# Three mixtures of experts: all rows through all experts, or only the routed rows in blocks of 128

## The chip, the cores and the metric

One core of a Trainium2 chip runs the whole program. The metric is device time in microseconds of one execution. The engines are TensorE (PE, its weight loads PEld), VectorE (DVE), ScalarE (ACT), GpSimd (POOL) and SyncE (SP, which issues most DMAs). Each works through its own instruction stream and waits on semaphores that the others raise.

## The reference

The input x is 2 x 512 rows of 128 numbers, in float32; a context of 2 x 77 rows goes with it. Four levels follow, each adding a gated attention to the context (the second with a self-attention inside its feed-forward part) and a gated mixture of experts. The mixtures of levels 1 to 3 have 8 experts with 512 hidden units, and each row uses its two best experts:

```
gate_probs = softmax(x1 @ Wg + bg);  topk_p, topk_i = top_k(gate_probs, 2)
comb = sum(one_hot(topk_i, E) * topk_p[..., None], -2)          # level 1 divides topk_p by its sum
h = gelu(einsum('bsd,edf->bsef', x1, W1) + b1)
y = einsum('bsef,efd->bsed', h, W2) + b2
moe_out = einsum('bse,bsed->bsd', comb, y)
```

Level 2 has a ninth choice (the row itself, without an expert) and no biases; level 3 has the tanh form of gelu and plain probabilities as weights. The reference multiplies every row by every expert and lets `comb` put zeros on six of the eight.

## The kernel before

Rows lie in 8 tiles of 128, four for each batch ("half"). Each engine's stream is written out by hand; the order of the code is the order of the work, and semaphores hold the engines together. The stages are: level 0 (attention and a mixture of another kind), cross-attention 1, self-attention, mixture 1, cross-attention 2 ("attention 2"), mixture 2, attention 3, mixture 3.

A mixture (`moe`) runs 16 pairs of an expert and a half in the order `MOE_ORDER`. On PE, `hidden(i)` (L1527) multiplies the 512 turned rows of the half (HTR, feature by row) by the first matrix in four matmuls of 512 columns; ACT applies gelu (L689); then 16 matmuls (L1543) make the expert's output for four tiles, in one of two PSUM banks. DVE (L1087) adds it to ACC, times the row's gate (GC). `hidden(i+1)` is issued before the second matrices of pair i. The weights of an expert, 512 KB, are one slot of the ring RINGW of 6; SP (L360) loads the next when a slot is free, 8 experts for a mixture. Between the pairs, at the places PREPARE_AT, VW_AT and NEXT_AT, stand the keys and values of the next attention and the turn of its first half.

A cross-attention (`cross_tiles`) runs units of 8 heads on one tile, 16 in attentions 2 and 3, as a pipeline over PE, DVE, ACT and POOL (L477 divides by the sum); `before[s]` are steps of DVE on the second half that belong to the mixture before. In its last steps the first half is normalized and turned for the next mixture.

## Time and profile before

| what | value |
|---|---|
| median of 3 runs | 948.68 us (943.76 to 1962.34) |
| the profiled execution | 943.48 us |
| its span, first to last instruction | 941.7 us |
| busy PE / DVE / ACT / POOL | 766.1 / 462.1 / 395.4 / 137.1 us |
| mean granted clock of TensorE | 0.902 |
| DMA | 38.48 MB, mean 41 GB/s |

The profile is of one execution. Busy time is the union of an engine's instructions; a group's mean is that of one instruction, which overlaps its neighbours, so that the mean times the count exceeds the busy time. One float32 matmul of the program leaves two records. The granted clock is a share of 2.4 GHz: 1.00 is that level, 0.50 is 1.2 GHz.

### The profile page before, as it was taken

To read this page: it belongs to the slowest core of one execution; us is meant where nothing else is said; L and a number is where in the kernel's file an instruction comes from. 1 tells how busy PE (TensorE), PEld (TensorE's weight loads), DVE (VectorE), ACT (ScalarE), POOL (GpSimd) and SP (SyncE) were. 2 spreads that over 40 slices of the span, in tenths; PEclk is the share of its full clock that TensorE was granted. 3 is DMA by queue.
4 is the path that set the end of the run, shared out by engine and by line. 5 is a ranking of instruction groups with operands and counts; after the bars stand their busy time and mean duration, and the time that the engine had idled before them with its cause. 6 is when DMAs were issued, how large, how long until landed. Compare 5 with 4: busy or idle time off the path is not lost.

```text
span 941.7 us, 12265 instructions
## 1 busy us (share of the span) xinstructions
PE 766.1 (81%) x4480; PEld 507.0 (54%) x4480; DVE 462.1 (49%) x1144; ACT 395.4 (42%) x942; POOL 137.1 (15%) x205
## 2 busy tenths in 40 slices
PE   2042589856779999799999768999999678899997
PEld 2030246635542333267677446767777458677775
DVE  6977923277776775262113589341121448432112
...
GB/s 356 57 1 0 0 45 179 6 1 2 128 223 51 2 3 1 135 1 1 31 38 46 67 1 1 1 1 23 45 23 78 12 1 1 1 1 1 45 12 12
DMA packets 16802, 38.48 MB, mean 41 GB/s; under 512 B 1174, under 2 KB 10707, under 8 KB 16483
## 3 DMA queue, kind: packets, MB, share of 16 engines
...
q8 instruction: 36, 0.59, 0.3%
q14 instruction: 24, 0.20, 0.1%
...
## 4 chain that ended last, share of the span: by engine, by line
PE 66%; DVE 24%; ACT 5%; issue 4%; DMA 1%; POOL 0%; SPq 0%; DVEq 0%; ACTq 0%; POOLq 0%
PE PS L1543 18%; PE PS L1527 18%; PE PS L1659 4%; PE PS L1354 3%; PE PS L1621 3%; DVE NTOP L1030 3%; PE PS L1649 3%; DVE MX L1162 2%; DVE BIG L1031 2%; PE PS L1310 2%; PE PS L1260 1%; DVE XH L787 1%; PE PS L1364 1%; PE PS L1502 1%; PE PS L1340 1%
## 5 line engine op out<-in xcount | busy, mean ns | idle before, releaser
L1543 PEld LDWEIGHTS PS<-RINGW,BIG 128*128 128x128 f32 x1536 | 178.8, 192 | 22.0 <-issue 22.0
L1543 PE MATMUL PS<-RINGW,BIG 128*128 128x128 f32 x1536 | 179.3, 275 | 0.3 <-PE PS L1543 0.3
L1087 DVE SCALAR_TENSOR_TENSOR ACC<-PS,GC,ACC 128x128 f32<-128x128 f32 x192 | 54.1, 344 | 252.1 <-PE PS L1543 222.9
L1527 PE MATMUL PS<-HTR,RINGW 128*128 128x512 f32 x384 | 175.5, 602 | 2.6 <-PE PS L1543 1.5
L689 ACT ACTIVATE BIG<-PS,Wt 128x512 f32<-128x512 f32 x128 | 86.5, 685 | 89.0 <-PE PS L1527 88.6
L1527 PEld LDWEIGHTS PS<-HTR,RINGW 128*128 128x128 f32 x384 | 70.2, 192 | 76.1 <-issue 75.9
L1162 DVE TENSOR_REDUCE MX<-PS 128x2 f32<-128x1024 f32 x64 | 78.5, 1226 | 25.5 <-PE PS L1621 23.7
L1354 PE MATMUL PS<-BIG 128*128 128x128 f32 x400 | 56.6, 293 | 8.7 <-DVE TMP L1212 3.1
L477 POOL TENSOR_TENSOR BIG<-BIG,REC 128x616 f32<-128x616 f32 x40 | 48.6, 1215 | 94.6 <-DVE REC L1040 94.6
L1354 PEld LDWEIGHTS PS<-BIG 128*128 128x128 f32 x400 | 51.2, 203 | 17.6 <-issue 10.6
L689 ACT ACTIVATE BIG<-PS 128x512 f32<-128x512 f32 x64 | 37.9, 598 | 38.3 <-PE PS L1527 37.8
L1649 PE MATMUL PS<-BIG 75*128 75x512 bf16 x128 | 44.7, 406 | 6.7 <-ACT BIG L742 2.4
L1621 PE MATMUL PS<-BIG 72*128 72x512 bf16 x128 | 43.2, 429 | 4.8 <-DVE RK L1137 2.4
L594 ACT ACTIVATE BIG<-BIG 128x308 f32<-128x308 f32 x40 | 18.5, 463 | 59.4 <-DVE BIG L1031 59.2
L1030 DVE TENSOR_REDUCE NTOP<-PS 128x8 f32<-128x616 f32 x32 | 25.6, 800 | 35.2 <-PE PS L1340 29.0
L742 ACT ACTIVATE BIG<-PS 128x512 f32<-128x512 f32 x64 | 34.9, 595 | 15.7 <-PE PS L1649 15.1
L600 ACT ACTIVATE BIG<-PS,NTOP 128x77 f32<-128x77 f32 x128 | 39.4, 324 | 0.0
L1364 PE MATMUL PS<-Ct,BIG 128*128 128x128 f32 x200 | 32.4, 299 | 7.1 <-ACT BIG L609 7.1
L1336 PE MATMUL PS<-BIG 32*128 32x308 f32 (+1 forms) x96 | 22.7, 577 | 14.8 <-ACT BIG L600 11.1
L609 ACT ACTIVATE BIG<-PS 128x384 f32<-128x384 f32 x80 | 30.8, 447 | 8.5 <-PE PS L1364 8.5
L460 POOL TENSOR_TENSOR BIG<-BIG,Ct 128x154 f32<-128x154 f32 (+2 forms) x20 | 14.1, 704 | 135.9 <-ACT BIG L565 135.9
L1260 PE MATMUL PS<-Ct,XH 128*128 128x128 f32 x80 | 16.1, 340 | 20.9 <-DVE XH L787 9.1
...
## 6 DMA issues: line engine op xcount, KB each, us to landing
RINGW<-up SPq DMA_DIRECT2D x40, 512.0 KB, 3.8
...
X<-x SPq DMA_DIRECT2D x1, 512.0 KB, 3.4
```

The lines of the kernel that those rows point to most:

```text
L477: nc.gpsimd.tensor_tensor(s, s, bc(REC[:, u % 4, :], C, 2), ALU.mult).then_inc(sem(f"p{k}_normed"), 1)
L600: ins = nc.scalar.activation(e, raw, ACT.Exp, bias=NTOP[:, s % 2, h:h + 1], accum_out=REC[:, s % 4, h:h + 1])
L689: nc.scalar.activation(HB[g % 2][:, ch, :], PS[:, ch, :], func, bias=col)\
L1030: st.do(v.tensor_reduce(ntop, raw, AX.X, ALU.max, negate=True))
L1087: ins = v.scalar_tensor_tensor(out=ACC[:, t, :], in0=PS[:, 4 + g % 2, j * D:(j + 1) * D], scalar=GC[:, t, e:e + 1], in1=ACC[:, t, :], op0= ...
L1162: v.tensor_reduce(MX[g % 2][:, 2 * (un % 2):2 * (un % 2) + 2, un // 2], PS[:, 2 * (i % 2):2 * (i % 2) + 2, :], AX.X, ALU.max, negate=True) ...
L1354: ins = mm(PS[:, 7, 0:D], x["pt"][u % 3][:, i * P:(i + 1) * P], x["vw"][:, t // HT, hh, i, :], start=(hh == 0 and i == 0), stop=(hh == per ...
L1364: ins = tp(PS[:, 4 + n, (i - 3 * n) * P:(i - 3 * n + 1) * P], x["sc"][u % 4][:, i * P:(i + 1) * P], ident)
L1527: mm(PS[:, ch, :], RINGW[:, slot, ch * P:(ch + 1) * P], HTR[:, cols(b)], start=True, stop=True)\
L1543: ins = mm(PS[:, 4 + g % 2, j * D:(j + 1) * D], HB[g % 2][:, ch, j * P:(j + 1) * P], RINGW[:, slot, F + ch * D:F + (ch + 1) * D], start=(c ...
L1621: ins = mm(PS[:, 2 * (i % 2) + x, :], QS[0:72, h, q0:q0 + P], KS[0:72, h, cols(b)], start=True, stop=True)
L1649: mm(PS[:, 4 + idx % 2, :], KS[0:75, h, k0:k0 + P], QS[0:75, h, cols(b)], start=True, stop=True)\
```

## The change

Each half of a mixture is now computed on routed rows. DVE finds each row's two experts (`route_shift`, `route_picks`), PE counts each row's rank among the rows of its expert with a triangle of ones (`half_ranks`), and DVE turns that into slots of 128 (`route_slots`): the first 128 rows of expert e go to block e, further ones to blocks 8 to 14, whose expert is looked up (`expert_int`). 512 rows with two experts each fill at most 15 blocks, and 15 are always run. POOL spreads the rows of XH into a DRAM buffer with 8 indirect DMAs (`dispatch`); SP loads them back, block by block (`load_rows`). PE turns four blocks at a time (`rows_turn`), multiplies each by its expert in 4 and 4 matmuls of 128 columns, DVE copies the result (YS), SP stores it, POOL gathers two rows for each row with 8 indirect DMAs (`bring`), and DVE adds them with their gates (`combine`). The weights carry the first bias in 4 more columns and are loaded once for each block, 30 times for a mixture; for blocks 8 to 14 SP reads the expert's number into a register first.

The first half is routed during the attention before, the second half among the first blocks. The first half's rows come back during blocks 15 to 29, the second half's during the first units of the next attention, where the `before` steps of DVE start at unit step 5 or 4 (they started at 0). The second bias is added in front, from the dense gates. Semaphores of the three attentions are shared; two buffers more lie in DRAM, filled once behind the loads of level 0.

```diff
+UPW = 2 * F + FC
+BLOCKS = 15
+ALL = B * BLOCKS
+LATER = BLOCKS - E
+ROWS = BLOCKS * P + N
...
-        MOE_ORDER = [(e, 0) for e in range(6)] + [(0, 1), (1, 1), (2, 1), (6, 0), (7, 0)] + [(e, 1) for e in range(3, E)]
-        BIAS_AT, PREPARE_AT, VW_AT, NEXT_AT = 4, 5, 9, 14
-        HALF_DONE = MOE_ORDER.index((E - 1, 0))
...
+        TURN_AT, LOGITS_AT, RANK_AT = {1: 1}, {1: 3}, {1: 6, 2: 1, 3: 1}
+        COMB_AT = (8, 12)
+        PREPARE_AT, VW_AT, NEXT_AT = {1: 9, 2: 6}, {1: 16, 2: 18}, 28
+        RETURN_AT, ROWS_AT = 24, {1: 11, 2: 9, 3: 9}
...
-            load_experts(E0, E0 + RING)
-            load_experts(E0 + RING, E0 + 3 * E)
...
+            def load_block(n):
+                k, b, i = n // ALL + 1, n % ALL // BLOCKS, n % BLOCKS
+                if i < E:
+                    src = up[E * (k - 1) + i]
+                else:
+                    if i == E:
+                        sp.wait_ge(sem("experts_known"), route(k, b) + 1)
+                    chosen = ROUTE[b].expert_int[0:1, i - E:i - E + 1]
+                    src = up[sp.value_load(chosen, min_val=0, max_val=E - 1) + E * (k - 1)]
+                if n >= RING:
+                    sp.wait_ge(sem("block_out"), n - RING + 1)
+                else:
+                    sp.wait_ge(sem("expert_used"), E0)
+                r = E0 + n
+                sp.dma_start(RINGW[:, r % RING, :], src).then_inc(sem(f"expert_loaded{r % RING}"), 16)
+            def load_rows(k, b):
+                sp.wait_ge(sem(f"dispatched{b}"), 16 * 2 * HT * k)
+                if k == 1:
+                    sp.wait_ge(sem("scores"), P)
+                if b:
+                    sp.wait_ge(sem("rows_turned"), 8 * (k - 1) + 4)
+                for n, (lo, hi) in enumerate(((0, 4), (4, 8), (8, BLOCKS))):
+                    src = rows[b][lo * P:hi * P, :].rearrange("(n p) d -> p n d", p=P)
+                    sp.dma_start(rows_in(k, lo, hi), src).then_inc(sem(f"rows_loaded{b}_{n}"), 16)
+            for n in range(RING):
+                load_block(n)
+            for k in (1, 2, 3):
+                load_rows(k, 0)
+                for i in range(ALL):
+                    n = ALL * (k - 1) + i
+                    if n + RING < 3 * ALL:
+                        load_block(n + RING)
+                    if i == ROWS_AT[k]:
+                        load_rows(k, 1)
+                    sp.wait_ge(sem("block_copied"), n + 1)
+                    b, m = i // BLOCKS, i % BLOCKS
+                    sp.dma_start(rows[b][m * P:(m + 1) * P, :], YS[n % 4]).then_inc(sem(f"block_stored{n % 4}"), 16)
...
+            def dispatch(k, b, t):
+                for i in range(2):
+                    at = bass.IndirectOffsetOnAxis(ap=ROUTE[b].slot_int[:, i, t:t + 1], axis=0)
+                    nc.gpsimd.indirect_dma_start(rows[b], at, XH[:, HT * b + t, :], None).then_inc(sem(f"dispatched{b}"), 16)
+            def dispatch_first(k, between):
+                pool.wait_ge(sem("slots_known"), route(k, 0) + 1)
+                for t in range(2):
+                    dispatch(k, 0, t)
+                if between:
+                    ln(1)
+                for t in range(2, HT):
+                    dispatch(k, 0, t)
+            def dispatch_second(k):
+                pool.wait_ge(sem("slots_known"), route(k, 1) + 1)
+                for t in range(HT):
+                    dispatch(k, 1, t)
+            def stored(k, b):
+                end = ALL * (k - 1) + BLOCKS * (b + 1)
+                for n in range(end - 4, end):
+                    pool.wait_ge(sem(f"block_stored{n % 4}"), 16 * (n // 4 + 1))
+            def bring(k, b, which):
+                for n in which:
+                    t, i = n // 2, n % 2
+                    at = bass.IndirectOffsetOnAxis(ap=ROUTE[b].slot_int[:, i, t:t + 1], axis=0)
+                    nc.gpsimd.indirect_dma_start(YG[k, b][:, t, i, :], None, rows[b], at).then_inc(sem(f"returned{b}"), 16)
...
+                if k > 1:
+                    transposed(1, HTR)
+                    half_exp(k, 1)
+                rows_out(0)
+                for n in range(ALL):
+                    act.wait_ge(sem("block_hidden"), base + n + 1)
+                    if k == 2:
+                        ins = nc.scalar.activation(HBLK[n % 2].rearrange("p c s -> p (c s)"), PS[:, 1 + n % 2, :], func)
+                    else:
+                        for ch in range(FC):
...
+            def combine(k, b):
+                ro = ROUTE[b]
+                dve.wait_ge(sem(f"returned{b}"), 16 * 2 * HT * k)
+                for i in range(2):
+                    for t in range(HT):
+                        to, y, gate = ACC[:, HT * b + t, :], YG[k, b][:, t, i, :], ro.gate[i][:, t:t + 1]
+                        if k == 2 and i == 0:
+                            ins = v.tensor_scalar(to, y, gate, None, ALU.mult)
+                        else:
+                            ins = v.scalar_tensor_tensor(out=to, in0=y, scalar=gate, in1=to, op0=ALU.mult, op1=ALU.add)
...
+            def blocks(k, after):
+                base = ALL * (k - 1)
+                if k > 1:
+                    route_shift(k, 1)
+                    route_picks(k, 1)
+                for i in range(ALL):
+                    n = base + i
+                    dve.wait_ge(sem("block_out"), n + 1)
+                    if n >= 4:
+                        dve.wait_ge(sem(f"block_stored{n % 4}"), 16 * (n // 4))
+                    v.tensor_copy(YS[n % 4], PS[:, 3 + n % 2, 0:D]).then_inc(sem("block_copied"), 1)
+                    if k == 1 and i == LOGITS_AT[k]:
+                        route_shift(k, 1)
+                    if k == 1 and i == LOGITS_AT[k] + 1:
+                        route_picks(k, 1)
+                    if i == RANK_AT[k]:
+                        route_slots(k, 1)
+                    if k in GATED and i - 3 in COMB_AT:
+                        add_bias(k, COMB_AT.index(i - 3))
+                    if RETURN_AT <= i < RETURN_AT + len(after):
+                        after[i - RETURN_AT](0)
...
+            def blocks(k, m, norms, next_m=None, next_norm=None):
+                base = ALL * (k - 1)
+                def rows_turn(g):
+                    b, at = g // 4, group_of(g)
+                    if at.start in (0, 4, 8):
+                        pe.wait_ge(sem(f"rows_loaded{b}_{at.start // 4}"), 16 * k)
+                    if g:
+                        pe.wait_ge(sem("rows_turned_ready"), 8 * (k - 1) + g)
+                    for n, i in enumerate(at):
+                        ins = tp(PS[:, 0, n * P:(n + 1) * P], rows_in(k, i, i + 1)[:, 0, :], ident)
+                    ins.then_inc(sem("rows_turned"), 1)
+                def first(n):
+                    b, i = n // BLOCKS, n % BLOCKS
+                    g = 4 * b + i // 4
+                    expert_ready(pe, E0 + base + n)
+                    pe.wait_ge(sem("rows_turned_ready"), 8 * (k - 1) + g + 1)
+                    if base + n >= 2:
+                        pe.wait_ge(sem("block_gelu"), base + n - 1)
+                    for ch in range(FC):
+                        ins = mm(PS[:, 1 + n % 2, ch * P:(ch + 1) * P], RINGW[:, ring_slot(base + n), ch * P:(ch + 1) * P],
+                                 XT[g % 2][:, (i % 4) * P:(i % 4 + 1) * P], start=True, stop=True)
+                    ins.then_inc(sem("block_hidden"), 1)
+                def second(n):
+                    pe.wait_ge(sem("block_gelu"), base + n + 1)
+                    if base + n >= 2:
+                        pe.wait_ge(sem("block_copied"), base + n - 1)
+                    for ch in range(FC):
+                        ins = mm(PS[:, 3 + n % 2, 0:D], HBLK[n % 2][:, ch, :],
+                                 RINGW[:, ring_slot(base + n), F + ch * D:F + (ch + 1) * D], start=(ch == 0), stop=(ch == FC - 1))
+                    ins.then_inc(sem("block_out"), 1)
+                if k > 1:
+                    turn(m, 1, XH, "xh_ready", norms)
+                    half_logits(k, 1, m)
+                rows_turn(0)
+                first(0)
+                for n in range(ALL):
+                    if n + 1 < ALL:
+                        first(n + 1)
+                    second(n)
+                    for g in range(1, 8):
+                        if n == turn_at(k, g):
...
+            def half_ranks(k, b):
+                pe.wait_ge(sem("picked"), route(k, b) + 1)
+                both = ROUTE[b].both
+                for t in range(HT + 1):
+                    at = PS[:, route_bank(k, b), 64 + t * E:64 + (t + 1) * E]
+                    for t2 in range(min(t + 1, HT)):
+                        ins = mm(at, TRI if t2 == t else ONES16, both[:, t2, :], start=(t2 == 0), stop=(t2 == min(t, HT - 1)))
+                ins.then_inc(sem("ranked"), 1)
```

What stands on PE at the end of attention 2 and in the first pairs of mixture 2, before (L1354 attention output, L1260 turn, L1514 logits):

```order
L1354 MATMUL PS<-BIG 128x128 x5
L1364 MATMUL PS<-Ct,BIG 128x128 x5
L1354 MATMUL PS<-BIG 128x128 x10
L1514 MATMUL PS<-Wt,HTR 128x9 x4
L1527 MATMUL PS<-HTR,RINGW 128x512 x8
L1543 MATMUL PS<-RINGW,BIG 128x128 x16
L1260 MATMUL PS<-Ct,XH 128x128 x4
L1514 MATMUL PS<-Wt,HTR 128x9 x4
L1527 MATMUL PS<-HTR,RINGW 128x512 x4
L1543 MATMUL PS<-RINGW,BIG 128x128 x16
```

And now (L1684 attention output, L1733 ranks, L1723 logits, L1747 turns of routed rows, L1758 first and L1767 second matrices):

```order
L1684 MATMUL PS<-BIG 128x128 x5
L1694 MATMUL PS<-Ct,BIG 128x128 x5
L1733 MATMUL PS<-RG,Ct 128x8 x14
L1684 MATMUL PS<-BIG 128x128 x10
L1577 MATMUL PS<-Ct,XH 128x128 x4
L1723 MATMUL PS<-Wt,HTR 128x9 x4
L1747 MATMUL PS<-Ct,Y 128x128 x4
L1758 MATMUL PS<-BIG,RINGW 128x128 x8
L1767 MATMUL PS<-RINGW,BIG 128x128 x4
L1747 MATMUL PS<-Ct,Y 128x128 x4
L1758 MATMUL PS<-BIG,RINGW 128x128 x4
L1767 MATMUL PS<-RINGW,BIG 128x128 x4
L1733 MATMUL PS<-RG,Ct 128x8 x14
```

The first matrices come after the logits of both halves and after the first turn of routed rows, which are loaded from DRAM into Y; a block has 4 and 4 matmuls of 128 columns, where a pair had 4 of 512 and 16 of 128.

What stands on POOL from the last unit of attention 2 on, before (L417 and L418 the norm, L453 clearing, L460 and L466 masks for attention 3):

```order
L417 TENSOR_SCALAR RS<-MV 128x4
L418 TENSOR_TENSOR RS<-RS,HALFNEG 128x4
L477 TENSOR_TENSOR BIG<-BIG,REC 128x616 x3
L417 TENSOR_SCALAR RS<-MV 128x4
L418 TENSOR_TENSOR RS<-RS,HALFNEG 128x4
L453 MEMSET BIG 128x2560 x2
L460 TENSOR_TENSOR BIG<-BIG,Ct 128x154
```

And now (L605 is L477 of before, L626 spreads rows, L573 clears, L584 and L590 are the masks):

```order
L605 TENSOR_TENSOR BIG<-BIG,REC 128x616 x3
L626 DMA rows<-XH,RG 2432x128 x4
L538 TENSOR_SCALAR RS<-MV 128x4
L539 TENSOR_TENSOR RS<-RS,HALFNEG 128x4
L626 DMA rows<-XH,RG 2432x128 x4
L573 MEMSET BIG 128x2560 x2
L626 DMA rows<-XH,RG 2432x128 x8
L584 TENSOR_TENSOR BIG<-BIG,Ct 128x154
```

The 8 spreading DMAs of the first half follow the last unit, with the second half's norm between them; the second half's 8 stand ahead of all masks.

What stands on SP when mixture 1 begins, before:

```order
L397 DMA BIG<-MTS 3x4x512 x7
L360 DMA RINGW<-up 128x1024 x24
L406 DMA out<-X 128x512 x2
L103 UNCONDITIONAL_BRANCH
```

And now (L499 weights, L493 an expert's number, L524 a block's result, L510 routed rows):

```order
L499 DMA RINGW<-up 128x1028
L524 DMA rows<-YT 128x128
L493 TENSOR_LOAD RG
L493 ISA x2
L499 ISA
L499 DMA RINGW<-up 128x1028
L524 DMA rows<-YT 128x128
L493 TENSOR_LOAD RG
L493 ISA x2
L499 ISA
L499 DMA RINGW<-up 128x1028
L524 DMA rows<-YT 128x128
L493 TENSOR_LOAD RG
```

The weights were 24 loads in a row, each waiting for a free slot only. Now each load stands ahead of a store that waits for a block's copy, and a register load stands ahead of seven of fifteen.

## Rows read from the trace of the kernel before

**Rows 1.** Stretches: PE, PEld, DVE, ACT, POOL busy, granted clock, DMA share, GB/s.
```profile
401.00:529.00 128.00, 125.57 (x725) 91.89 (x724) 36.81 (x140) 51.80 (x81) 15.38 (x17) 0.99 0.09 30
529.00:598.50 69.50, 51.36 (x327) 38.32 (x326) 53.70 (x123) 42.14 (x182) 23.24 (x22) 0.83 0.02 8
598.50:727.70 129.20, 127.16 (x753) 95.07 (x752) 32.17 (x121) 47.68 (x83) 20.07 (x42) 1.00 0.09 29
727.70:816.20 88.50, 67.34 (x418) 55.68 (x418) 49.89 (x117) 50.22 (x196) 21.90 (x20) 0.92 0.02 7
816.20:937.00 120.80, 118.36 (x677) 85.85 (x676) 27.19 (x108) 47.65 (x70) 1.26 (x2) 1.00 0.03 12
```

**Rows 2.** The page's costliest groups.
```profile
L1543 PE MATMUL PS<-RINGW,BIG 128*128 128x128 f32 x1536 | 179.3, 275 | 0.3 <-PE PS L1543 0.3
...
L1527 PE MATMUL PS<-HTR,RINGW 128*128 128x512 f32 x384 | 175.5, 602 | 2.6 <-PE PS L1543 1.5
...
L477 POOL TENSOR_TENSOR BIG<-BIG,REC 128x616 f32<-128x616 f32 x40 | 48.6, 1215 | 94.6 <-DVE REC L1040 94.6
```

**Rows 3.** Chain of waits in mixture 2: start us, us, what.
```profile
625.36 3.44 PE PS L1527 x8
628.80 3.57 PE PS L1543 x32
```

**Rows 4.** Instructions in order of time, and groups by shape: short matmuls.
```profile
577.34 1.38 PE L1354 MATMUL PS<-BIG 128*128 128x128 f32 x10
578.55 0.71 PE L1364 MATMUL PS<-Ct,BIG 128*128 128x128 f32 x5
...
L1456 PE MATMUL PS<-IDB,BIG 128*128 128x128 bf16 x64 | 5.4, 232 | 0.0
```

**Rows 5.** Instructions in order of time, and groups by shape: ACT.
```profile
416.24 1.26 ACT L689 ACTIVATE BIG<-PS,Wt 128x512 f32<-128x512 f32 x2
...
L600 ACT ACTIVATE BIG<-PS,NTOP 128x77 f32<-128x77 f32 x128 | 39.4, 324 | 0.0
```

**Rows 6.** Stretches of the opening load; DMA queues of 250:262; page; line 360.
```profile
4.00:6.00 2.00, 0.00 (x0) 0.00 (x0) 1.71 (x11) 0.00 (x0) 0.23 (x1) 1.00 0.80 236
16.00:18.00 2.00, 0.00 (x0) 0.00 (x0) 1.83 (x4) 0.72 (x1) 0.00 (x0) 1.00 1.11 479
...
DMA packets 2935, 2.88 MB, mean 240 GB/s; under 512 B 122, under 2 KB 2935, under 8 KB 2935
...
RINGW<-up SPq DMA_DIRECT2D x40, 512.0 KB, 3.8
...
L360 SPq DMA_DIRECT2D RINGW<-up x40: 327/328/1437, 5.1 to 882.0; - x40
```

**Rows 7.** Groups by shape: POOL.
```profile
L418 POOL TENSOR_TENSOR RS<-RS,HALFNEG 128x4 f32<-128x4 f32 x16 | 16.6, 1038 | 1.3
...
L460 POOL TENSOR_TENSOR BIG<-BIG,Ct 128x1232 f32<-128x1232 f32 x2 | 4.5, 2258 | 48.4 <-ACT BIG L565 48.4
```

**Rows 8.** End of attention 2: in order of time, chain of waits, stretch.
```profile
588.24 0.20 DVE L1040 RECIPROCAL REC<-REC 128x8 f32<-128x8 f32 x1
...
586.11 2.48 PE L1354 MATMUL PS<-BIG 128*128 128x128 f32 x10 [3.08 <-DVE TMP L1212]
589.44 0.60 PE L1260 MATMUL PS<-Ct,XH 128*128 128x128 f32 x4
...
598.53 6.97 PE PS L1527 x16
...
586.00:590.00 4.00, 3.89 (x21) 3.92 (x22) 2.78 (x6) 2.27 (x11) 1.22 (x1) 0.57 0.00 0
```

**Rows 9.** The end in order of time; the DMA issues.
```profile
937.33 1.13 DVE L1087 SCALAR_TENSOR_TENSOR ACC<-PS,GC,ACC 128x128 f32<-128x128 f32 x4 [2.99 <-PE PS L1543]
...
out<-X SPq DMA_DIRECT2D x2, 256.0 KB, 2.0
```

**Rows 10.** End of self-attention in order of time.
```profile
387.99 0.66 PE L1260 MATMUL PS<-Ct,XH 128*128 128x128 f32 x4
```

612 lines of the change are left out of this document (385 added, 227 removed).

## The prediction

> **What bounds the kernel now.** I read the stretches first [rows 1]. The three later mixtures run at 401 to 529, 598.5 to 727.7 and 816.2 to 937 us. In each the matmul engine is busy 98% of the time at a granted clock of 0.99 to 1.00, while DVE, ACT and the DMA engines have room to spare (DVE 27 to 37 us of 121 to 129; DMA share 0.09 at most). So the matmul engine bounds these 378 us. In the two attentions between them it is busy 74 to 76% and DVE 56 to 77%: there a chain over several engines bounds.
>
> The costliest groups name the work [rows 2]: second matrices 179.3 us, first matrices 175.5 us. The chain of waits shows one expert on one half [rows 3]: 3.44 us for 8 records of 512 columns, then 3.57 us for 32 records of 128. That is 7.01 us per pair of expert and half, 16 pairs per mixture, 112.2 us of the 121 to 129. The rest, 9 to 17 us, is routing, biases and the next attention's keys and values. Every pair costs its 7.01 us on all 512 rows, though two experts of eight want each row.
>
> **What is removed and added on the matmul engine.** Removed: 48 pairs x 7.01 = 336.5 us, all on the path.
>
> Added: 90 blocks (15 for each half, for each mixture). A block is 4 matmuls of 128 columns and 4 more, thus 16 records. A record of this shape costs 3.57/32 = 0.1116 us [rows 3], so a block is 1.79 us and 90 are 160.7. The block's rows must be turned first: 5 transposes take 0.71 us [rows 4], 90 take 12.8. Counting ranks takes 14 small bf16 matmuls for a half; the 64 bf16 ones of 128 columns took 5.4 us [rows 4], so 1.2 us, and three of the six lie inside a mixture: 3.6. Together 177.1, **net -159.4 us**. The work beside the experts stays as it is.
>
> **Engines that could take over in a block.** ACT: two activations of 512 columns with a bias took 1.26 us and one of 77 columns 0.324 [rows 5]. Four of 128 lie between 4 x 0.16, a quarter of the former, and 4 x 0.37, the latter with 51 columns more; I take 1.2 us. They run behind the 1.79 us of the block before and the next, so they are hidden with about 0.3 us to spare, and the copies of turned rows (one of 512 columns for four blocks) meet turns of the same length on the matmul engine. The second mixture has one activation a block, with more room. DVE: a block's copy to the row tile is one operation of the size of which four took 1.13 us [rows 9], 0.28 us in 1.79; hidden.
>
> **Weights.** Each block loads 514 KB, and its result leaves with 64 KB: 0.59 MB every 1.79 us, 330 GB/s. The burst at the start ran at 479 GB/s in one stretch and 236 in another, and lines under 2 KB at 240 on average around 256 us [rows 6]. Six slots give a load about four blocks, 7.2 us, against 3.8 us to landing [rows 6]. I cost this at 2 us a mixture, for the moments when 0.98 MB of rows is loaded for the second half; its cover is those four blocks, and if it is gone each block waits for its bytes (rival A).
> SP also reads an expert's number into a register for 7 of 15 blocks. No row shows this. Lower bound: nothing. Upper bound: the 2.0 us in which 256 KB land [rows 9]; with two issues of 0.33 us [rows 6] an SP turn is then 2.7 us for 7 blocks, 6.1 us behind in total, which the slots nearly absorb. I take nothing, and up to 3 us per half for the range.
>
> **The price of an indirect DMA on POOL.** The trace has none. Lower bound: an SP issue, 0.33 us [rows 6]; upper bound: the largest multiply of POOL, 2.26 us [rows 7]. POOL's ordinary instructions are 1.04 and 1.22 us, the former on only 4 elements [rows 2, 7], so I take **1.2 us**, plus 2.0 us to landing [rows 9]. There are 96, 8 for each half to spread its rows and 8 to bring them back. Those that nothing covers are the 8 that start each mixture and the last 8.
>
> **The starts.** Before, mixture 2 began on a tile that was ready. Now its first block waits for a chain. XH is turned at 589.4 to 590.7 [rows 8]; then on DVE 3 small operations, ACT's exponential, 13 more, the ranks, and 13 to the slots. A small DVE operation lasts 0.20 us [rows 8]; with its start I take 0.25. With the attention's own instructions between them the slots are there at about 603, 4.5 us after 598.5 [rows 8]. Then POOL: 8 x 1.2 + 1.3 (the norm between them) = 10.9; landing 2.0; SP loads the first 256 KB of rows, 2.6 (an issue, a landing and a little for the small lines); turn and copy 1.2. Sum 4.5 + 10.9 + 2.0 + 2.6 + 1.2 = 21.2, less 1.7 for the copy and turns that ran there before: **+19.5 us**, twice. The second half's turn and logits fit inside. In mixture 1, the first half's XH was turned at 387.99 [rows 10]; moved three steps earlier, it puts the slots at about 397, and 9.6 + 2.0 + 2.6 + 1.2 bring the first block to 412.4 against 401: **+11.4**.
>
> **Inside the mixtures.** Mixture 1 routes its second half among the blocks. At block 6 the matmul engine waits for picks that DVE issued after block 5 (19 x 0.25 = 4.8 us): a stall of 4. The slots are then there 22.4 us after the first block's start (6 blocks 10.7, turn, logits and ACT's change of tables 3.5, the stall 4, 17 operations 4.2), the rows at 22.4 + 9.6 + 2.0 + 2.6 = 36.6. They are wanted after block 13, at 25.1 + 3.5 + 4 + 0.7 = 33.3: a stall of 3.3 more. Mixtures 2 and 3 pick during the start's idle time and need nothing. POOL's 40 masks for the third attention move behind the dispatch of 8, but the matrices that read them moved from pair 9 to block 18: covered. After each idle start the clock is at the lower level for some microseconds: the same 10 records took 2.48 us at 586, granted clock 0.57 [rows 8], for 1.38 at 577 [rows 4]. That is 2 us a mixture.
>
> **The attentions.** In attentions 2 and 3 DVE adds back the second half: 8 x 0.28 = 2.3 us, and its turn now comes just ahead of unit 8 instead of unit 3: 5 us each for both. Self-attention gives up 1 us to the routing inside it. POOL's 8 returns lie beside units that start about 3 to 5 us apart and hold 1.22 us of POOL: covered, or their price falls on units 0 to 2.
>
> **The end.** Before, the last additions (1.13 us) began at 937.3, 4.4 us before the span's end [rows 9]. Now stand in their place: copy 0.3, store 0.3 + 2.0, 8 x 1.2, landing 2.0, combination 8 x 0.28 = 2.3. That is 16.5 - 1.1 = **+15.4**.
>
> **Sum**: -159.4 + 11.4 + 39.0 + 7.3 + 6.0 (DMA) + 6.0 (clock) + 11.0 (attentions) + 15.4 = -63.3. The profiled execution took 943.5 us (span 941.7), 5 below the median of the runs, 948.7. 943.5 - 63.3 = **880 us**.
>
> **Rivals.**
> A. *The weights set the pace.* At the 240 GB/s of the small lines a block's 0.59 MB takes 2.46 us: 0.67 x 72 blocks (the 18 first are loaded ahead) = +48, **928 us**. For it: 330 GB/s wanted. Against: up to 479 GB/s in the opening burst, with long lines as here [rows 6]. 13%.
> B. *POOL is dear.* An indirect DMA at 2.26 us or more, the upper bound, adds 32 x 1.06 = 34 us: **914**; the stalls in mixture 1 grow too. The mechanism that could do it here: POOL writes its requests beside a DVE that copies a block every 1.79 us and works 77% of attention 2 [rows 1]. Against: POOL's multiplies there keep their 1.22 us beside that DVE [rows 2]. 14%. The Trainium skill (SBUF — State Buffer, the box on the "DVE blocks DMA" trap) says that GpSimd's DMAs need descriptors that it writes itself, and that a VectorE copy in a two-port mode shuts it out of the port meanwhile. It gives 620 ns alone and about 3100 ns beside a copy; at 3.1 us each for 1.2, 32 of them would add 61 us, by the sum 941. No row here shows it.
> C. *The slower end: the clock.* Short matmuls with a wait in each block could keep the engine at 1.2 GHz. Then a block takes 3.58 us and 90 add 161: **1041 us**. It decides from 63/1.79 = 35 blocks at the lower level. For it: the granted clock fell to 0.83 in attention 2, where the engine is busy 74% [rows 1]. Against: with small tiles and a busy engine it was 0.92 to 1.00. 3%. The Trainium skill (TensorE: Matmul & The Clock Gate, HAM oscillation) warns of this for thin tiles that wait for DMA.
> D. *The chains are shorter.* Slots ready with the attention's end, POOL at 0.5 us, no queueing: -22 for 32 DMAs, -9 for slots, -6: **843 us**. 10%.
>
> **How the numbers follow.** 60% for the forecast. Its own range: POOL at 0.45 to 1.8 us gives -24 and +19, the attentions 0 to 20 for 11, the stalls half to double: 846 to 915. The range is **842 to 930**, which takes in D and most of A and B. Faster by over 2% (below 925 on the profiled time, which is about what can be told from no change) holds the forecast, D, most of B and part of A: 0.85; within 2%: 0.10; slower: 0.05, C and the far ends of A and B together.
>
> **What would show it.** In the changed profile: the second-matrix group and the first-matrix group at about 80 us each; mixtures of 75 to 85 us from first block to last; idle time of the matmul engine before each first row turn of 10 to 20 us, ended by a DMA; POOL's indirect DMAs about 1.2 us apart; 20 us from the last matmul to the end; the granted clock near 1.00 inside the mixtures. A block period above 2.2 us with first matmuls waiting for RINGW means A; DMAs over 2 us apart mean B; a clock near 0.5 means C. I am wrong in the sum if the starts cost under 8 or over 30 us.

## The result and the profile after

| kernel | median us | runs | ratio to before, 95% interval |
|---|---|---|---|
| before | 946.97 | 4 | |
| changed | 900.02 (897.44 to 901.98) | 4 | 0.9513 [0.9467, 0.956] |
| best of the experiments (`e11_spaced_store_first`) | 875.95 (870.80 to 880.33) | 4 | 0.9261 [0.9198, 0.9323] |

One of before's four runs took 1962 us; the ratio leaves it out. The change saves 5%. The forecast was 880 us with a range of 842 to 930, so direction and range held and the sum was 20 us too good. In profiled executions, 943.5 us went to 901.3, that is 42 us, where the sum had 63.

The page of the changed kernel: engine, busy time, share, instructions; then the DMA totals and the queue of POOL's DMAs.

```profile
span 899.4 us, 12378 instructions
PE 634.2 (71%) x4221; PEld 469.1 (52%) x4222; DVE 465.8 (52%) x1218; ACT 366.4 (41%) x1043; POOL 230.7 (26%) x297
...
DMA packets 54244, 93.91 MB, mean 104 GB/s; under 512 B 5526, under 2 KB 38099, under 8 KB 53859
...
q0 software_dynamic: 3072, 6.30, 2.3%
```

The costliest groups that answer to [rows 2], with busy us, mean ns, and idle time ahead:

```profile
L1767 PE MATMUL PS<-RINGW,BIG 128*128 128x128 f32 x720 | 104.4, 292 | 23.2 <-ACT BIG L902 13.4
...
L1758 PE MATMUL PS<-BIG,RINGW 128*128 128x128 f32 x720 | 104.4, 291 | 5.4 <-issue 4.5
...
L902 ACT ACTIVATE BIG<-PS,RINGW 128x128 f32<-128x128 f32 x240 | 68.5, 372 | 54.3 <-PE PS L1758 41.6
...
L626 POOL DMA_INDIRECT rows<-XH,RG x48 | 47.3, 986 | 116.8 <-DVE RG L1354 104.2
...
L655 POOL DMA_INDIRECT BIG<-rows,RG x48 | 46.1, 961 | 102.1 <-DMA rows<-YT 90.2
```

354.8 us of expert matmuls became 208.8. The idle time ahead of L1767, ended by ACT, was not in the forecast. The stretches answer to [rows 1]. They are cut here at the end of each mixture's last block and at the first block of the next: start of mixture 1, mixture 1, attention 2 with the start of mixture 2, mixture 2, attention 3 with the start of mixture 3, mixture 3, the end. Columns: span, PE, PEld, DVE, ACT, POOL busy, granted clock, DMA share, GB/s.

```profile
400.57:412.88 12.31, 1.12 (x6) 0.75 (x5) 6.75 (x16) 0.73 (x2) 8.42 (x8) 0.64 0.38 112
412.90:504.20 91.30, 75.56 (x605) 72.34 (x606) 25.48 (x105) 47.40 (x145) 27.39 (x30) 0.93 0.70 211
504.20:610.20 106.00, 65.31 (x354) 48.61 (x353) 66.94 (x199) 43.24 (x186) 44.79 (x42) 0.71 0.09 26
610.20:690.50 80.30, 74.31 (x620) 73.43 (x620) 16.39 (x67) 29.28 (x53) 29.48 (x50) 0.94 0.74 230
690.50:798.40 107.90, 72.84 (x496) 65.97 (x495) 64.67 (x193) 50.53 (x200) 39.11 (x38) 0.85 0.11 33
798.40:878.90 80.50, 69.35 (x544) 67.91 (x544) 15.55 (x57) 40.24 (x130) 15.26 (x16) 0.86 0.68 207
878.90:899.40 20.50, 0.01 (x1) 0.00 (x0) 3.32 (x10) 0.00 (x0) 7.55 (x8) 0.57 0.18 55
```

With before cut at the same points (its mixture 1 ended at 529.2, mixture 3 at 937.2) the account closes:

| stage | before | after | difference | in the sum |
|---|---|---|---|---|
| start of mixture 1 (with 1 us in self-attention) | | | +11.9 | +12.4 |
| three mixtures | 128.2 + 129.2 + 121.0 | 91.3 + 80.3 + 80.5 | -126.3 | -140.1 |
| attention 2 and start of mixture 2 | 69.3 | 106.0 | +36.7 | +24.5 |
| attention 3 and start of mixture 3 | 88.5 | 107.9 | +19.4 | +24.5 |
| the end | 4.5 | 20.5 | +16.0 | +15.4 |
| sum | | | -42.3 | -63.3 |

So two places hold the error: 13.8 us inside the mixtures, and 12.2 in attention 2, of which attention 3 gives 5.1 back.

**Where a mixture loses time.** In order of time, the second half's dispatch in mixture 3, an engine at a time (start us, duration, instruction, idle time before and what ended it). POOL, then DVE, ACT and PE:

```profile
809.50 0.96 POOL L626 DMA_INDIRECT rows<-XH,RG  x1 [17.09 <-DVE RG L1354]
810.76 0.95 POOL L626 DMA_INDIRECT rows<-XH,RG  x1 [0.30 <-issue]
...
818.34 0.96 POOL L626 DMA_INDIRECT rows<-XH,RG  x1 [0.30 <-issue]
...
813.83 0.29 DVE L1395 COPY YT<-PS 128x128 f32<-128x128 f32 x1 [3.38 <-remote]
821.05 0.29 DVE L1395 COPY YT<-PS 128x128 f32<-128x128 f32 x1 [6.94 <-remote]
...
816.72 0.60 ACT L890 ACTIVATE BIG<-PS 128x512 f32<-128x512 f32 x1 [4.73 <-remote]
820.29 1.92 ACT L902 ACTIVATE BIG<-PS,RINGW 128x128 f32<-128x128 f32 x7 [2.97 <-remote]
...
811.53 0.60 PE L1747 MATMUL PS<-Ct,BIG 128*128 128x128 f32 x4
811.97 1.06 PE L1758 MATMUL PS<-BIG,RINGW 128*128 128x128 f32 x8
812.86 1.06 PE L1767 MATMUL PS<-RINGW,BIG 128*128 128x128 f32 x8
813.76 1.06 PE L1758 MATMUL PS<-BIG,RINGW 128*128 128x128 f32 x8
821.48 0.79 PE L1767 MATMUL PS<-RINGW,BIG 128*128 128x128 f32 x2 [6.67 <-ACT BIG L902]
```

ACT's copy at 816.72 waits for one thing only, the transposes of L1747, whose records end at 812.13. "Remote" says that the release came at a moment when the profile shows no instruction that gave it. The semaphore updates in the trace do show it: TensorE's update for those transposes came at 816.69, 4.6 us after the recorded end, and those for the first matrices of the two blocks behind them at 820.26 and 821.12, 7.2 and 6.3 us late. Its updates came more than 1 us late in six stretches of the execution, and those are the six in which POOL issues eight indirect DMAs back to back inside a mixture (439 to 447, 468 to 476, 625 to 634, 661 to 669, 812 to 821, 854 to 861). Before has none in its mixtures, and no update of DVE, ACT or POOL is over 0.5 us late in either trace.

What is late, the work or the word of it? The trace shows some of both. The updates come in bunches: 821.03 and 821.12 here, four from 447.19 to 447.47 in mixture 1; each bunch begins 1.6 to 1.7 us after the end of the eighth DMA. A group of 8 records takes 0.9 us, so of the work behind the second update of such a pair all but 0.1 us was done before the first: there the word is late. In at least two of the stretches the work itself is also held: at a granted clock of 1.00, single matmuls of one group start 0.4 to 0.8 us apart in place of 0.11. The group of 631.01:

```profile
631.01 0.50 PE L1758 MATMUL PS<-BIG,RINGW 128*128 128x128 f32 x3
632.05 0.27 PE L1758 MATMUL PS<-BIG,RINGW 128*128 128x128 f32 x1 [0.55 <-issue]
632.75 0.27 PE L1758 MATMUL PS<-BIG,RINGW 128*128 128x128 f32 x1 [0.43 <-issue]
```

How the lateness divides between the two isn't shown. "Held back" stands for both below.

### The profile page after: what moved, and what is told of

Its sections match the earlier page's. It is cut to its first block and busy times, and to the rows that moved or that the text cites. A ratio compares the mean times of both kernels' runs of the same rounds, so it can differ in the third digit from the quotient of the medians.

```text
span 899.4 us, 12378 instructions
## 1 busy us (share of the span) xinstructions
PE 634.2 (71%) x4221; PEld 469.1 (52%) x4222; DVE 465.8 (52%) x1218; ACT 366.4 (41%) x1043; POOL 230.7 (26%) x297
## 2 busy tenths in 40 slices
DMA packets 54244, 93.91 MB, mean 104 GB/s; under 512 B 5526, under 2 KB 38099, under 8 KB 53859
## 3 DMA queue, kind: packets, MB, share of 16 engines
q0 software_dynamic: 3072, 6.30, 2.3%
## 5 line engine op out<-in xcount | busy, mean ns | idle before, releaser
L1395 DVE COPY YT<-PS 128x128 f32<-128x128 f32 x90 | 25.7, 291 | 190.8 <-PE PS L1767 136.5
L1767 PE MATMUL PS<-RINGW,BIG 128*128 128x128 f32 x720 | 104.4, 292 | 23.2 <-ACT BIG L902 13.4
L1767 PEld LDWEIGHTS PS<-RINGW,BIG 128*128 128x128 f32 x720 | 95.3, 206 | 25.5 <-ACT BIG L902 16.8
L1758 PE MATMUL PS<-BIG,RINGW 128*128 128x128 f32 x720 | 104.4, 291 | 5.4 <-issue 4.5
L1758 PEld LDWEIGHTS PS<-BIG,RINGW 128*128 128x128 f32 x720 | 95.6, 206 | 8.1 <-issue 7.4
L902 ACT ACTIVATE BIG<-PS,RINGW 128x128 f32<-128x128 f32 x240 | 68.5, 372 | 54.3 <-PE PS L1758 41.6
L1684 PE MATMUL PS<-BIG 128*128 128x128 f32 x400 | 62.5, 313 | 27.8 <-DVE TMP L1527 17.5
L626 POOL DMA_INDIRECT rows<-XH,RG x48 | 47.3, 986 | 116.8 <-DVE RG L1354 104.2
L1684 PEld LDWEIGHTS PS<-BIG 128*128 128x128 f32 x400 | 57.0, 222 | 36.5 <-issue 29.7
L655 POOL DMA_INDIRECT BIG<-rows,RG x48 | 46.1, 961 | 102.1 <-DMA rows<-YT 90.2
L605 POOL TENSOR_TENSOR BIG<-BIG,REC 128x616 f32<-128x616 f32 x40 | 48.6, 1217 | 78.0 <-DVE REC L1261 77.8
L787 ACT ACTIVATE BIG<-BIG 128x308 f32<-128x308 f32 x40 | 18.5, 462 | 64.0 <-DVE BIG L1252 62.4
L1694 PE MATMUL PS<-Ct,BIG 128*128 128x128 f32 x200 | 35.4, 318 | 11.1 <-ACT BIG L802 10.9
L961 ACT ACTIVATE BIG<-PS 128x512 f32<-128x512 f32 x64 | 34.9, 595 | 16.2 <-PE PS L2021 15.6
```

Source lines behind the costliest of these rows:

```text
L605: nc.gpsimd.tensor_tensor(s, s, bc(REC[:, u % 4, :], C, 2), ALU.mult).then_inc(sem("x_p_normed"), 1)
L626: nc.gpsimd.indirect_dma_start(rows[b], at, XH[:, HT * b + t, :], None).then_inc(sem(f"dispatched{b}"), 16)
L655: nc.gpsimd.indirect_dma_start(YG[k, b][:, t, i, :], None, rows[b], at).then_inc(sem(f"returned{b}"), 16)
L902: ins = nc.scalar.activation(HBLK[n % 2][:, ch, :], PS[:, 1 + n % 2, ch * P:(ch + 1) * P], func, bias=RINGW[:, ring_slot(base + n), 2 * F ...
L1684: ins = mm(PS[:, 7, 0:D], x["pt"][u % 3][:, i * P:(i + 1) * P], x["vw"][:, t // HT, hh, i, :], start=(hh == 0 and i == 0), stop=(hh == per ...
L1694: ins = tp(PS[:, 4 + n, (i - 3 * n) * P:(i - 3 * n + 1) * P], x["sc"][u % 4][:, i * P:(i + 1) * P], ident)
```

## The experiments

Theory H: POOL's indirect DMAs hold TensorE back. Its rivals: the weights and rows come too slowly (W), the traffic of these transfers does it (T), the late updates are an effect of profiling (N).

**1. Without the inner indirect DMAs.**

```diff
 def dispatch_second(k):
-    for t in range(HT):
-        dispatch(k, 1, t)
 def bring(k, b, which):
-    for n in which:
+    for n in which[:0] if b == 0 else which:
```
(what waited for them waits for the slots, or for nothing)

> Leaves out the 48 of 96 indirect DMAs that POOL issues inside the three mixtures (the second half's dispatch and the first half's return), so the second half is computed from rows that were never routed and the first half's return adds stale data; all matmuls, weights and stores stay. In the changed kernel's trace the six stretches of about 11 us in which these DMAs are issued hold 2 to 3 blocks where 5 to 6 would fit, 6 us lost in each. Theory H (TensorE is held back while POOL issues indirect DMAs): the stretches close, mixtures shrink by 8 to 12 us each with the clock that fell after the stalls, time 865 to 875. Rival W (the weights and rows do not come faster): stalls stay at other places, 893 to 901. Rival N (the late updates are only in the profile): 897 to 901 without a profile.

869.50 us (867.12 to 872.27), ratio 0.9197 [0.915, 0.9243]. Its mixtures, which answer to the second, fourth and sixth of the stretches above:

```profile
414.30:494.20 79.90, 72.75 (x605) 71.02 (x606) 25.51 (x105) 47.86 (x145) 11.94 (x14) 0.93 0.76 228
...
602.30:673.10 70.80, 70.80 (x621) 70.62 (x621) 16.45 (x67) 29.42 (x53) 14.16 (x34) 0.97 0.79 244
...
782.00:845.70 63.70, 63.33 (x544) 62.31 (x544) 15.56 (x57) 40.52 (x130) 0.00 (x0) 0.96 0.76 245
```

Together 214.4 us for 252.1, no late update left, and the median of the four runs is 30 us lower. So N falls in the form that only the record is late; every run on record lists a span and a clock, so whether an execution with the profiler off is held up too isn't shown. W falls, since all the weights still pass, at more GB/s, and TensorE never waits for RINGW. The 37.7 us are of one trace of the changed kernel: where other experiments below keep all six bursts (6 to 10), the mixtures take 246 to 253 us, 32 to 38 over these.

**2. Small weights.**

```diff
 to = RINGW[:, r % RING, :]
+if n >= RING:
+    to, src = to[:, 0:16], src[:, 0:16]
```

> Leaves out most of each expert load inside the mixtures (16 of 1,028 columns are loaded, so the matmuls use old weights); the indirect DMAs stay. It takes away some 42 MB of the 94. Theory H in its pure form (the issue of indirect DMAs alone holds TensorE): the six stretches stay, 895 to 901. Theory HW (it needs the indirect DMAs and the weight traffic together): the late updates go and it comes out as without those DMAs, 865 to 875. Rival W (loads alone set the pace): also 865 to 875, but then the kernel without the inner indirect DMAs would not be faster.

903.14 us (901.17 to 903.81), ratio 0.9536 [0.9492, 0.9579]. 50.4 MB moved in place of 93.9, and nothing was gained. The late updates stand in the same six stretches, up to 7.1 us. H holds in its pure form: the bytes of the weights have no part in it, and are not the bound either. The number of loads and of packets (54,244) stayed the same.

**3. Plain DMAs.**

```diff
 if b:
+    nc.gpsimd.dma_start(rows[b][n * P:(n + 1) * P, :], XH[:, HT * b + t, :])
+    continue
```
(and likewise for the first half's return)

> The same 48 transfers inside the mixtures, same bytes and same engine, but as plain DMAs of fixed row blocks in place of indirect ones (so rows are not routed for the second half, nor returned for the first). Theory H (descriptors written by POOL for indirect rows are what holds TensorE): as without them, 865 to 875. Rival T (the traffic of these transfers is what holds it): as the changed kernel, 895 to 901.

868.23 us (866.62 to 873.00), ratio 0.919 [0.9141, 0.924]. The same packets and bytes went over the same queue (3,072 packets, 6.30 MB), POOL spent 0.55 us on each, and no update of TensorE was late. T falls: it is the indirect form, not how much it moves. The plain DMAs also go to consecutive rows and hold POOL for less time; which part of the indirect form does the harm wasn't taken apart.

**4. Spaced.** Pairs in place of eight in a row:

```diff
 for t in range(HT):
+    pool.wait_ge(sem("block_out"), ALL * (k - 1) + 4 + 2 * t)
     dispatch(k, 1, t)
```
(return: `18 + 2 * t`; `RETURN_AT` 25, `ROWS_AT` 12)

> All 96 indirect DMAs, but those inside the mixtures go out in pairs, one pair per two blocks (block 4, 6, 8, 10 and 18, 20, 22, 24), where now eight go out back to back; the second half's rows are loaded at block 12, the return is added from block 25. Theory H by density (a backlog that builds up after two or three DMAs): stalls shrink to under 1 us per pair, 875 to 885. Theory H by count (each DMA costs TensorE its 0.7 us wherever it stands): 895 to 903. Rival N or W: 898 to 903, with 1 to 3 us more for the later return.

898.95 us (895.48 to 901.56), ratio 0.9486 [0.9438, 0.9534]: by the total, the count theory. The trace says otherwise. POOL and PE around the same place in mixture 3:

```profile
819.03 0.96 POOL L626 DMA_INDIRECT rows<-XH,RG  x1 [1.31 <-PE PS L1770]
820.29 0.96 POOL L626 DMA_INDIRECT rows<-XH,RG  x1 [0.30 <-issue]
822.77 0.96 POOL L626 DMA_INDIRECT rows<-XH,RG  x1 [1.51 <-PE PS L1770]
824.03 0.96 POOL L626 DMA_INDIRECT rows<-XH,RG  x1 [0.30 <-issue]
...
820.54 1.06 PE L1761 MATMUL PS<-BIG,RINGW 128*128 128x128 f32 x8
821.43 1.06 PE L1770 MATMUL PS<-RINGW,BIG 128*128 128x128 f32 x8
822.32 1.06 PE L1761 MATMUL PS<-BIG,RINGW 128*128 128x128 f32 x8
823.22 1.08 PE L1770 MATMUL PS<-RINGW,BIG 128*128 128x128 f32 x8
```

Blocks follow every 1.79 us beside the DMAs. DVE's copies of blocks 2 to 8 come over 9.5 us (814.8 to 824.3), and in the first experiment over 9.4 (793.7 to 803.1). In mixture 1 the eight of the dispatch still went back to back, since its slots are known only at block 7. What the spacing won was lost again: TensorE waited 6.4 us in mixtures 2 and 3 each for rows of the second half that now came late, and the return was late by 2 to 3.

**5. Spaced in time.** The same with the readers set to it:

```diff
-RETURN_AT, ROWS_AT = 24, {1: 11, 2: 9, 3: 9}
+RETURN_AT, ROWS_AT = {1: 24, 2: 25, 3: 25}, {1: 11, 2: 10, 3: 10}
-return max(before, first - 4) + (k == 1 and g == 4)
+return max(before, first - 4) + (g == 4)
 # dispatch_second, k > 1: pool.wait_ge(sem("block_out"), ALL * (k - 1) + 3 + 2 * t)
 # bring, b == 0: ... + 16 + ((0, 2, 3, 5) if k == 1 else (0, 2, 4, 6))[t]
```

> All 96 indirect DMAs and the whole computation. The ones inside the mixtures go out in pairs with a block or more between (second-half dispatch of mixtures 2 and 3 from blocks 3, 5, 7, 9; first-half return from blocks 16, 18, 20, 22, in mixture 1 from 16, 18, 19, 21), and what reads them is set so that it need not wait: rows of the second half loaded at block 10, their turn one block later, the return added from block 25 in mixtures 2 and 3. The first spaced kernel ran mixtures 2 and 3 at the block pace of the one without these DMAs, but lost 6.4 us in each to rows that came late and 2 to 3 us to a late return. Density theory (only a burst of more than two or three holds TensorE): mixtures 2 and 3 at 71 to 73 us and 64 to 66 us, mixture 1 3 to 5 us shorter than 91, 870 to 880. Count theory (0.7 us per DMA): 893 to 900.

881.05 us (877.93 to 882.53), ratio 0.9282 [0.9232, 0.9332], with the whole computation in place: 1 us outside the forecast, and far from the count theory's. Mixtures 86.4, 76.5 and 65.8 us: the third as forecast, mixture 2 some 4 us longer. So it is density. Laid beside the copies of experiment 1, block by block, the pairs of number 4 with 1.3 us or more between cost at most 0.2 us, those of mixture 3's dispatch here, with 0.9 to 1.8 between, 0.4; the four places where four DMAs still went back to back cost 0.4 to 1.9 us (blocks 16 to 20 of mixture 3: 8.4 us for 7.5); eight in a row, in the changed kernel, cost 4 to 10.

**6. Two guesses on attention 2's start.** The next half's turn behind the last block:

```diff
-PREPARE_AT, VW_AT, NEXT_AT = {1: 9, 2: 6}, {1: 16, 2: 18}, 28
+PREPARE_AT, VW_AT, NEXT_AT = {1: 9, 2: 6}, {1: 16, 2: 18}, 29
```

> One number: the turn of the next stage's first half stands behind the last block's second matmuls, not ahead of them. In mixture 1 TensorE waited 3.44 us at 501.4 for that half's XH with the last block's second matmuls queued behind. Theory (the last block, its store and so the return into attention 2 hang on this turn): last block 2 to 3 us earlier, attention 2's returns begin at 505 to 506 instead of 508.7, total -2 to -4: 896 to 898. Rival (DVE's copy of the last block waits for DVE anyway, or SP's queue sets the store): 899 to 901.

902.22 us (899.33 to 903.44), ratio 0.9499 [0.945, 0.9548]: nothing. The last block ended at 501.9, and the stretch behind it took 110.6 us for 106.0; the sum of both stayed (88.0 + 110.6 for 91.3 + 106.0).

```diff
+sp.dma_start(rows[b][m * P:(m + 1) * P, :], YS[n % 4])...
 if n + RING < 3 * ALL:
     load_block(n + RING)
-sp.dma_start(rows[b][m * P:(m + 1) * P, :], YS[n % 4])...
```

> In SP's queue each block's store goes ahead of the load of the block six later. In the changed kernel the last store of mixture 1 was issued at 504.6 behind a load of 514 KB and POOL had its landing at 508.7. Theory (stores wait behind loads): the landing comes 1.5 to 2 us earlier, returns with it, -2 to -4 in all: 896 to 898. Rival (store landing is its own latency): 899 to 902.

900.70 us (897.94 to 906.12), ratio 0.9512 [0.9457, 0.9567]. The returns began 2.6 us after the last block, for 4.5, and attention 2 with its start took 100.8 us, for 106.0; but the total shows nothing, since mixture 2 took 83.9 for 80.3. In the five other traces with the same attention 2 (experiments 1 to 5) that stretch took 105.6 to 108.2. Inconclusive alone.

**7. Free return.** Leaves out the returns of the second halves of mixtures 1 and 2, and runs their chain early:

```diff
-HOOK_AT = {1: 0, 2: 5, 3: 4}
+HOOK_AT = {1: 0, 2: 1, 3: 1}
 def bring(k, b, which):
-    for n in which:
+    for n in which[:0] if b and k < 3 else which:
```

> Leaves out the 16 indirect DMAs that return the second halves of mixtures 1 and 2 (stale rows are added), and runs their chain on DVE (add, norm, residual, norm) right at units 1 to 3 of attentions 2 and 3 instead of units 5 to 7 and 4 to 5. Attention 2 took 93.7 us against 69.5 before; its extra is 11.6 us of idle time of TensorE and 27 us more at 1.2 GHz. Theory R (the late return puts 12 us of DVE work right ahead of unit 8, TensorE idles 9 us at 527 to 536 and the clock falls): attention 2 falls to 72 to 78, total 878 to 885. Rival Q (the routing chain of the next mixture inside the attention, 5.4 us of idle at 577 to 583 and DVE's load, is what lengthens it): attention 2 stays at 85 to 90, total 893 to 899.

903.50 us (898.49 to 909.72), ratio 0.9531 [0.9461, 0.9601]; attention 2 with its start 106.5 us; the total lies above both forecasts. My theory R falls as I had put it: the return is not what lengthens it, alone.

**8. Warm.** 128 idle matmuls:

```diff
+def warm(n):
+    for _ in range(n):
+        mm(PS[:, 6, 0:P], w("L2x_Wk")[:, 0:P], w("L2x_Wk")[:, 0:P], start=True, stop=True)
...
+if k == 2 and s < TURN_STEP[k]:
+    warm(16)
```

> Adds 128 matmuls of 128 columns that write a free bank and that nobody reads: 16 ahead of the turn at the end of mixture 1 and 16 after each of the steps 0 to 6 of attention 2, where TensorE mostly waits for DVE, ACT or POOL; 14 us of work at 2.4 GHz, 28 at 1.2. Attention 2 ran 51 of its 93.7 us at 1.2 GHz against 24 of 69.5 before, and TensorE was busy 12 us longer on about the same work. Theory C (the idle stretches let the clock fall, and that is half of attention 2's loss): under 35 us at 1.2 GHz and the stage from last block to first block of mixture 2 falls from 106 to 96 to 101 us, total 890 to 896. Rival (the chains on DVE set the pace and the added matmuls only stand in front of the real ones): stage 108 to 116, total 902 to 910.

903.94 us (902.55 to 905.73), ratio 0.9566 [0.9519, 0.9614]. The mean granted clock in the stretch rose from 0.71 to 0.87, and the stretch grew to 110.9 us. The forecast of theory C failed: this way of raising the clock loses. But the edit also puts TensorE's own work in the way (busy 80.9 us for 65.3). The first five units fell 9.2 us behind the changed kernel, and 3.6 of that came back by unit 10; so what a higher clock alone is worth isn't shown.

**9. Narrow.** The second half's chain on 16 of 128 columns:

```diff
-ins = v.bn_stats(ST6[:, t, :], src[:, t, :])
+ins = v.bn_stats(ST6[:, t, :], src[:, t, 0:WIDE[0]])
```
(and so in the four other steps; `WIDE[0]` is 16 in attention 2's steps on the second half)

> Leaves out seven eighths of the elements of the second half's chain on DVE inside attention 2 (add back, statistics, norm, gain, residual, norm, each on 16 of 128 columns); the indirect DMAs, their waits and the order stay. This chain is 12 us of DVE time between 523.6 and 540.6, and the kernel with the free return showed that its place alone changes nothing. Theory D (the length of the chain, on DVE ahead of unit 8, is what TensorE waits for): the 9 us of idle time at 536 shrink to 2 to 4 and the stage from last block to first block falls from 106 to 95 to 99 us, total 889 to 894. Rival (latency of the returns, the ping-pong with POOL and the clock): 103 to 107, total 897 to 901.

898.24 us (895.65 to 902.23), ratio 0.9491 [0.9442, 0.9539]; the stretch 102.6 us, the idle time 5.23 for 9.05. By the total this is the rival, but the edit did less than it was meant to: DVE's operations hardly shorten with their columns. The first of the chain, in the changed kernel and here:

```profile
523.57 2.90 DVE L1371 SCALAR_TENSOR_TENSOR ACC<-BIG,RG,ACC 128x128 f32<-128x128 f32 x8 [1.08 <-DMA BIG<-rows,RG]
...
528.47 2.01 DVE L1377 SCALAR_TENSOR_TENSOR ACC<-BIG,RG,ACC 128x16 f32<-128x16 f32 x8 [0.55 <-DMA BIG<-rows,RG]
```

DVE's work in the stretch fell by 3.7 us (63.3 for 66.9), of 11.8 us in the chain, and the stretch by 3.4: nearly one for one. So theory D isn't refuted; the other 8 us were never taken away.

**10. Free return and early turn.** As 7, with `TURN_STEP[2]` 4 for 7 and `QUERY_STEP[2]` 5 for 7; attention 3 keeps the changed kernel's order.

> As the kernel with the free return (the 16 indirect DMAs of the second halves of mixtures 1 and 2 left out, stale rows added), but in attention 2 the turn of the second half stands at step 4 and its query at step 5 (7 and 7 in the changed kernel; its chain on DVE again at units 1 to 3), and attention 3 keeps the order of the changed kernel. Counted from the last block of mixture 1, the 16 units' normalizations in attention 2 stood at 8.1 to 71.1 us in the changed kernel and at 8.8 to 61.1 before; the ten us are lost between the sixth and the eighth unit (25.8 to 44.6 us, before 30.2 to 36.2), and the free return alone kept 35.7 to 43.2 between the seventh and eighth. Theory P (return chain, turn and query stand in a row ahead of unit 8, and it takes both, an early chain and an early turn, to be rid of the ten us): unit 8 at 35 to 38, unit 16 at 59 to 63, last block to first block of mixture 2 in 95 to 98 us instead of 106, total 890 to 894. Rival (DVE's added work and the routing chain set the attention's length): unit 16 at 68 to 71 again, total 898 to 904.

898.17 us (892.31 to 901.02), ratio 0.9502 [0.9459, 0.9546]. The median is the rival's. The profiled execution is the fastest of the four (892.3). In it the stretch took 98.2 us and unit 16 came at 64.6, between the two forecasts. POOL's normalizations of units 7, 8 and 9 in the changed kernel:

```profile
538.50 1.22 POOL L605 TENSOR_TENSOR BIG<-BIG,REC 128x616 f32<-128x616 f32 x1 [1.47 <-DVE REC L1261]
548.82 1.22 POOL L605 TENSOR_TENSOR BIG<-BIG,REC 128x616 f32<-128x616 f32 x1 [9.10 <-DVE REC L1261]
553.40 1.22 POOL L605 TENSOR_TENSOR BIG<-BIG,REC 128x616 f32<-128x616 f32 x1 [3.37 <-DVE REC L1261]
```

and of this one:

```profile
546.33 1.22 POOL L604 TENSOR_TENSOR BIG<-BIG,REC 128x616 f32<-128x616 f32 x1 [2.32 <-DVE REC L1260]
548.43 1.22 POOL L604 TENSOR_TENSOR BIG<-BIG,REC 128x616 f32<-128x616 f32 x1 [0.88 <-DVE REC L1260]
551.96 1.22 POOL L604 TENSOR_TENSOR BIG<-BIG,REC 128x616 f32<-128x616 f32 x1 [2.32 <-DVE REC L1260]
```

Counted from the last block of mixture 1:

| unit | before | changed | free return | free and early |
|---|---|---|---|---|
| 6 | 30.2 | 25.8 | 32.2 | 34.0 |
| 8 | 36.2 | 44.6 | 43.2 | 39.6 |
| 16 | 61.1 | 71.1 | 71.6 | 64.6 |

**11. Spaced, and stores first.** Number 5 with the return at `(0, 3, 5, 7)` in mixtures 2 and 3, and stores ahead of loads:

> The kernel that spaced its inner indirect DMAs in time (881.1), with two changes: the first half's return in mixtures 2 and 3 goes out from blocks 16, 19, 21, 23 (in the trace four went back to back and TensorE lost 2.3 and 2.4 us there), and each store goes ahead of the load in SP's queue. Density theory: 2 us less in mixtures 2 and 3 each, 876 to 879. Rival (the later last pair delays the return, or the stores bring nothing): 880 to 883.

875.95 us, ratio 0.9261, the best version that computes everything; its interval [0.9198, 0.9323] lies below the changed kernel's. Its stretches, which answer to those of the changed kernel:

```profile
416.30:501.80 85.50, 75.01 (x605) 72.97 (x606) 25.48 (x105) 47.53 (x145) 27.39 (x30) 0.90 0.71 224
501.80:602.60 100.80, 63.24 (x354) 47.85 (x353) 67.64 (x199) 42.95 (x186) 44.83 (x42) 0.74 0.10 29
602.60:678.80 76.20, 72.42 (x620) 71.55 (x620) 16.42 (x67) 29.38 (x53) 29.40 (x50) 0.96 0.74 239
...
787.90:853.80 65.90, 64.38 (x544) 62.43 (x544) 15.59 (x57) 40.36 (x130) 15.25 (x16) 0.97 0.74 252
```

The mixtures are as in number 5 (85.5, 76.2, 65.9 for 86.4, 76.5, 65.8), so the later return brought nothing: the single gaps of 2.3 us that it was to save are mostly made up within the next block. The 5 us are attention 2's, 100.8 for 108.2, as with the stores alone (100.8). Two traces with it and none without show this length for the whole computation, so I take the order of SP's queue as the likely cause; the intervals of 5 and 11 overlap, and it is not proved.

## Why the prediction was right in sign and 20 us off

- **Matmuls, -159.4: right.** Without the bursts (experiment 1) the mixtures took 214.4 us for 378.4: -164.0. A block takes 1.79 us, as summed. That the whole agrees so well is in part luck: mixture 1 gave 48.3 us, the others 58.4 and 57.3, for 53.1 each. The sign I gave for it, groups of 80 us, was wrongly stated: a run of 8 records counts 1.06 us by their modelled ends though the next starts after 0.89, which makes 95 for 90 blocks, and with the lower clock the groups read 104.4.
- **The mis-sized term: what holds a mixture up.** The sum had 7.3 + 6.0 (DMA) + 6.0 (clock) = 19.3 us. Measured are 378.4 - 159.4 = 219.0 to 252.1, 33.1 us. Its causes were wrong too. The forecast priced the indirect DMAs by POOL's time and took those inside a mixture as covered. They cost POOL nothing that matters and the mixtures 37.7 us in the traces, 30 in the medians (experiment 1). The weights, for which I had 6.0, cost nothing (experiment 2).
- **The clock.** I expected it near 1.00 in the mixtures and 6.0 us of loss. By the stretches it is at most (1 - 0.93) x 91.3 + 0.06 x 80.3 + 0.14 x 80.5 = 22 us, since a low clock costs nothing while TensorE idles; with spacing, 14. Experiment 1 has 10 by the same rows, so 12 of the 22 go with the stalls, and are in their 37.7.
- **The starts: right.** TensorE idled 10.4 us ahead of mixture 1's first turn, ended by the rows' load, and +11.9 us stand for +11.4. Mixtures 2 and 3 began 18.5 us after their attention's last matmul, where before 0.6 lay between: +17.9 for +19.5. The parts of mixture 2's: slots 1.0 us (I had 4.5), POOL 11.4 (10.9), landing and load 4.2 (4.6), turn and copy 1.9 (1.2):

```profile
600.44 1.12 PE L1577 MATMUL PS<-Ct,XH 128*128 128x128 f32 x4 [8.72 <-DVE XH L1008]
...
608.39 1.12 PE L1747 MATMUL PS<-Ct,Y 128*128 128x128 f32 x4 [4.28 <-DMA Y<-rows]
```

- **The price on POOL, 1.2 us: right.** 0.96 us and 0.30 to the next. Rival B asked for DMAs over 2 us apart inside the mixtures; inside a burst none is. The Trainium skill's page "SBUF — State Buffer" (the "DVE blocks DMA" box) says that POOL can't write descriptors while DVE runs an operation that takes both ports, such as a float32 copy from SBUF to SBUF. The trace shows no such delay, 0.94 to 1.26 us each for all 96; but DVE's copies beside the bursts read PSUM, so that the box's own case isn't tested there. The harm was done to TensorE.
- **Attention 2, +5: too small by 14** (36.7 less the start's 17.9 is 18.8). After the last block the first five units run faster than before, then unit 8 comes 8.4 us later: the second half's return, its chain on DVE, its turn and its query stand in a row ahead of it, where before turn and query came by step 5. To free the return alone gives nothing; to take 3.7 us out of DVE's part gives 3.4; to free the return and turn early gives 5 us at unit 8 and 6.5 at unit 16, in one trace. The remaining 3.5 us, and a 5.4 us wait near the end (at 582.9; before, 3.1 at that place) where routing's small operations stand on DVE ahead of the attention's own, I have not taken apart. **Attention 3** had +19.4 for 24.5, 1.5 of it in the attention itself, for 5: that this gave part of attention 2's error back was luck.
- **The end: right**, 16.0 us for 15.4.
- **Rivals.** A (weights) is out by experiment 2, B by the DMAs' distance, C by a clock of 0.86 to 0.94 in the mixtures. D was right on the slots (1.0 us after the attention's last matmul) and wrong on POOL, 0.96 us for 0.5.

What stays open: why indirect DMAs hold TensorE back and plain ones from the same queue do not, and what must stand beside them. The eight ahead of mixture 1 (396.3 to 406.7) go out without a break too, and four and four ahead of the others; TensorE's few updates beside them (400.59, 601.57, 604.13) are at most 0.02 us late. Mixture 1's dispatch still goes back to back in number 11, because its slots are known only at block 7; it was not spaced in any run.
